# Graph layer on one core: every product of the last stage in plain fp32, from thirteen buffers

## The reference

```python
def _lap_mul(A, x):
    d = 1.0 / jnp.sqrt(jnp.sum(A, axis=-1))
    return d[:, None] * (A @ (d[:, None] * x))

z = leaky_relu(_lap_mul(A, x) @ W1 + b1, 0.1)
d2 = maximum(sq[:, None] + sq[None, :] - 2.0 * (z @ z.T), 0)     # sq = sum(z*z)
S = exp(-sqrt(d2 + 1e-10) / 2)
S = where(rank of S in its row < 4, S, 0)
x = _layernorm(x + _lap_mul(S + A, x) @ W2 + b2)
```

## Time and profile before

| | |
|---|---|
| median without a profile | 2692.08 us (3 runs) |
| span of the profiled execution | 2759.5 us |
| TensorE busy in it | 2482.6 us (90%) |
| VectorE busy | 2319.8 us (84%) |
| ScalarE busy | 1606.7 us (58%) |
| GpSimd busy | 1195.4 us (43%) |
| moved by DMA | 718.58 MB, 260 GB/s in the mean |

### The profile page before, as it was taken

One profiled execution on the slowest core, in us unless ns is written; L12 is line 12 of the kernel. 1 busy time (PEld: TensorE's weight loads), 2 busy tenths in 40 slices (PEclk: granted clock), 3 DMA queues, 4 the chain that ended last, 5 costly groups with the idle time before them and its releaser, 6 DMA issues.

```text
span 2759.5 us, 29107 instructions
## 1 busy us (share of the span) xinstructions
PE 2482.6 (90%) x9356; PEld 1722.4 (62%) x9356; DVE 2319.8 (84%) x1411; ACT 1606.7 (58%) x1905; POOL 1195.4 (43%) x987
## 2 busy tenths in 40 slices
PE   1367999999999998899999999999999987888978
PEld 0133444444677776578787877778787764666655
DVE  7998899977788888999999999999999773666766
ACT  0000000000477767999989899899988763555655
POOL 0000000000000000377778878788878956666760
PEclk9688999999999999999999999999999988999989
DMA  9999999995899960146555655555655688988975
GB/s 385 421 402 408 398 421 421 421 421 215 320 349 342 338 226 7 35 141 183 151 163 138 179 142 175 140 170 149 174 143 167 182 309 343 347 324 320 345 295 208
DMA packets 147949, 718.58 MB, mean 260 GB/s; under 512 B 19025, under 2 KB 26961, under 8 KB 86609
## 3 DMA queue, kind: packets, MB, share of 16 engines
q1 hardware_dynamic: 124384, 670.49, 65.6%
q0 software_dynamic: 18800, 37.77, 5.7%
q10 hardware_dynamic: 4608, 8.39, 0.8%
HBM read 680.40 MB, written 36.18 MB: 260 GB/s over the span
## 4 chain that ended last, share of the span: by engine, by line
PE 56%; issue 10%; ACT 10%; DVE 9%; DMA 7%; POOL 3%; another core or an unknown queue 3%; SPq 0%; ACTq 0%; POOLq 0%; DVEq 0%
PE PS L767 17%; PE PS L866 5%; PE PS L868 5%; PE PS L867 5%; DMA ring<-at 4%; ACT R L1141 3%; PE PS L834 3%; PE PS L910 3%; PE PS L921 3%; PE PS L911 3%; PE PS L830 2%; PE PS L831 2%; ACT ah_t L1191 2%; DVE R L1621 2%
## 5 line engine op out<-in xcount | busy, mean ns | idle before, releaser
L1299 POOL TENSOR_TENSOR al<-ring,ah 128x1024 fp32r<-128x1024 f32 x264 | 644.0, 2441 | 180.5 <-ACT ah L1112 168.7
L1621 DVE MAX8 R<-R 128x8 f32<-128x8192 f32 x64 | 555.9, 8685 | 68.1 <-ACT R L1141 67.9
L1141 ACT ACTIVATE R<-PS 128x1024 f32<-128x1024 f32 x512 | 518.1, 1018 | 114.1 <-PE PS L874 83.1
L1624 DVE FIND_INDEX8 R<-R,R 128x8 uint32<-128x8192 f32 x64 | 555.9, 8685 | 0.3 <-issue 0.3
L1272 POOL CAST zst<-zh 128x128 fp32r<-128x128 f32 (+1 forms) x64 | 26.2, 410 | 1113.2 <-DVE zl L1556 811.5
L866 PE MATMUL PS<-zh,zst 128*128 128x512 f32 x1024 | 407.3, 398 | 28.6 <-ACT PS L1127 12.7
L868 PE MATMUL PS<-zh,zst 128*128 128x512 f32 x1024 | 400.4, 391 | 0.0
L867 PE MATMUL PS<-zl,zst 128*128 128x512 f32 x1024 | 400.1, 391 | 0.0
L1456 POOL DMA_INDIRECT R<-xs_dram,R x256 | 279.7, 1093 | 145.2 <-issue 75.5
L1127 ACT ACTIVATE PS<-R 128x1024 f32<-128x1024 f32 x310 | 318.0, 1026 | 6.6
L1046 ACT ACTIVATE tiny<-rowsum 128x4 f32<-128x4 f32 x16 | 3.3, 205 | 481.2 <-DVE rowsum L1491 481.2
(11 more groups left out here) (177 smaller groups left out, 4469.9 us busy)
## 6 DMA issues: line engine op xcount, KB each, us to landing
R<-at SPq DMA_DIRECT2D x152, 1024.0 KB, 13.3
ring<-at SPq DMA_DIRECT2D x148, 1024.0 KB, 9.5
ring<-at SPq DMA_DIRECT2D x264, 512.0 KB, 3.9
cache<-at SPq DMA_DIRECT2D x117, 1024.0 KB, 20.2
raw_sq<-at SPq DMA_DIRECT2D x21, 1024.0 KB
raw_z<-at SPq DMA_DIRECT2D x20, 1024.0 KB
raw_ring<-at SPq DMA_DIRECT2D x20, 1024.0 KB
acc_dram<-R POOLq DMA_DIRECT2D x78, 256.0 KB, 5.7
```

Of the source, the lines that this page charges most:

```text
L1141: act.activation(score[j % 2][:, c * EC:(c + 1) * EC].rearrange("p (b c) -> p b c", b=2), pair(first, j, c), ACT.Copy).then_inc(copied, 1)
L1299: pool.tensor_tensor(al[:, k % SPLIT], raw[k % RAW], ah[:, k % SPLIT].bitcast(F32), ALU.subtract)\
L1621: v.max(top[:, j], score[j % 2]).then_inc(dve3, 1)
L1624: v.max_index(place[:, j], top[:, j], score[j % 2]).then_inc(placed, 1)
```

## The change

All 124 quads of the last stage are multiplied as the plain ones were.
- `round_t`, `rest_t`, the two subtractions on GpSimd, `ah_t`, `al_t` and their semaphores are gone. A quad's product waits for its load and for x.
- For h < 14 x comes from `xs_t`, 32 KB per partition in the place of `zh`. It is filled from `xp_dram`, which holds the scaled x of a group in one piece. In the loop one store of it takes the place of the stores of the two halves, and SP waits for both stores before it loads the next rows of x into `xg`. GpSimd's wait for the stores of the halves is gone; the halves are still made, for the pieces.
- `RAW_T` is 13: four buffers in `R1`, four in the place of `zl`, one over `sqn`, four in the ring. The load of quad u waits for the product of quad u - 13. The opening sequence of SP's loads is written out anew, by which part of `z` and of the ring is free. `ACC_AT` moves from (9, 20, 40) to (16, 27, 47).
- The last chain of small steps starts where it did, with no subtraction between its steps.

The diff, without the lines that only remove semaphores and names:

```diff
-RAW_T = 6
-BY_POOL = 2
-RESTS = 2
+RAW_T = 13
+CHAIN_AT = 2
...
-OPEN_T, SUM_AFTER, ACC_AT = 6, 4, (9, 20, 40)
+OPEN_T, SUM_AFTER, ACC_AT = 6, 4, (16, 27, 47)
...
-        ah_t = [sb(f"ah_t{k}", [P, TB, BC], F32R, at=top_of["ring"] + k * SLOT * 4) for k in range(2)]
-        al_t = [sb("al_t0", [P, TB, BC], F32R, at=top_of["ring"] + 2 * SLOT * 4),
-                sb("al_t1", [P, TB, BC], F32R, at=top_of["R1"] + 3 * SLOT * 4)]
+        xs_t = sb("xs_t", [P, T, D], at=top_of["zh"])
+        raw_t = [R1[:, k * SLOT:(k + 1) * SLOT].rearrange("p (k c) -> p k c", c=BC) for k in range(4)]
+        raw_t += [sb(f"raw_z{k}", [P, TB, BC], at=top_of["zl"] + k * SLOT * 4)[:, :, :] for k in range(4)]
+        raw_t.append(sb("raw_sq", [P, TB, BC], at=top_of["sqn"])[:, :, :])
+        raw_t += [sb(f"raw_ring{k}", [P, TB, BC], at=top_of["ring"] + k * SLOT * 4)[:, :, :] for k in range(4)]
...
-                        dst = xh_dram[bass.ds(g, 1)].rearrange("o p t d -> p (o t) d")
-                        sp.dma_start(dst, xgh_g[:, :, :].bitcast(F32)).then_inc(s_split, 16)
-                        dst = xl_dram[bass.ds(g, 1)].rearrange("o p t d -> p (o t) d")
-                        sp.dma_start(dst, xgl_g[:, :, :].bitcast(F32)).then_inc(s_split, 16)
+                        dst = xp_dram[bass.ds(g, 1)].rearrange("o p t d -> p (o t) d")
+                        sp.dma_start(dst, xg).then_inc(s_xp, 16)
                     if k == RAW + (NP0 // 2 if first else 0):
                         sp.wait_ge(s_xg, 16 * (g + 1))
+                        sp.wait_ge(s_xp, 16 * (g + 1))
                         sp.dma_start(xg, x[:, bass.ds((g + 1) * GT, GT)]).then_inc(s_xn, 16)
...
             def load_t(u):
                 b, h = tail[u]
-                if u >= RAW_T and plain[u - RAW_T]:
+                if u >= RAW_T:
                     sp.wait_ge(prod_t, u - RAW_T + 1)
-                elif u >= RAW_T:
-                    wait_rest(sp, u - RAW_T)
                 sp.dma_start(raw_t[u % RAW_T], at[b, h]).then_inc(ld_t[u % RAW_T], 16)
...
+                sp.dma_start(xs_t[:, g * GT:(g + 1) * GT], xp_dram[g]).then_inc(s_xs[g], 16)
+
+            def wait_z_free(chunks):
+
+                sp.wait_ge(gram, NE * (T - 1) + chunks)
+
+            sp.wait_ge(s_xp, 16 * (G - 1))
             sp.wait_ge(placed, T - 1)
...
+            load_t(0)
+            wait_z_free(1)
+            load_xs(0)
+            load_t(1)
             load_t(2)
-            sp.wait_ge(gram, NE * T)
+            wait_z_free(2)
+            load_xs(1)
             load_t(3)
+            load_t(4)
+            wait_z_free(4)
             load_xs(2)
-            load_t(4)
+            load_t(5)
+            load_xs(3)
+            wait_z_free(6)
+            load_t(6)
+            wait_z_free(8)
+            load_t(7)
+            load_t(8)
+            load_xs(4)
             sp.wait_ge(prodb, pieces_before(G - 1))
-            load_t(5)
+            for u in range(9, RAW_T):
+                load_t(u)
+            load_xs(5)
+            load_xs(6)
...
-                if plain[u]:
+                pe.wait_ge(ld_t[u % RAW_T], 16 * (u // RAW_T + 1))
+                if h >= LAST:
                     pe.wait_ge(xg_ok, chain_of(G - 1, False))
...
+                else:
+                    pe.wait_ge(s_xs[h * TB // GT], 16)
                 for k in range(TB):
...
+                    of_x = xg[:, (h * TB + k) % GT] if h >= LAST else xs_t[:, h * TB + k]
+                    i = pe.matmul(bank, of_x, raw_t[u % RAW_T][:, k], start=from_zero and k == 0,
+                                  stop=last and k == TB - 1, skip_group_check=True)
                 i.then_inc(prod_t, 1)
...
             for u in range(len(tail)):
-                if not plain[u]:
-                    round_t(u)
...
-            for u in range(BY_POOL):
-                pool.wait_ge(rnd_t, u + 1)
-                pool.tensor_tensor(al_t[u % 2][:, :, :], raw_t[u % RAW_T], ah_t[u % 2][:, :, :].bitcast(F32),
-                                   ALU.subtract).then_inc(al_pool, 1)
...
-                if not plain[u]:
-                    rest_t(u)
```

More of the change, by code:

```diff
@@ L126, in plan_tail, with build @@
     return quads
-def build(nc, x, at, W1, b1, W2, b2, consts, out, xs_dram, xh_dram, xl_dram, acc_dram):
+def build(nc, x, at, W1, b1, W2, b2, consts, out, xs_dram, xp_dram, acc_dram):
     loads, products, two = plan_ab()
@@ L284, in build @@
         spare = R2[:, (B - 1) * BC:B * BC]
[L285 to L292, removed]
-        ah_t = [sb(f"ah_t{k}", [P, TB, BC], F32R, at=top_of["ring"] + k * SLOT * 4) for k in range(2)]
-        al_t = [sb("al_t0", [P, TB, BC], F32R, at=top_of["ring"] + 2 * SLOT * 4),
-                sb("al_t1", [P, TB, BC], F32R, at=top_of["R1"] + 3 * SLOT * 4)]
+        xs_t = sb("xs_t", [P, T, D], at=top_of["zh"])
[3 more added lines that the diff above has]
+        raw_t += [sb(f"raw_ring{k}", [P, TB, BC], at=top_of["ring"] + k * SLOT * 4)[:, :, :] for k in range(4)]
+        assert len(raw_t) == RAW_T
         bt = [N]
@@ L376, in build @@
         flushed = sem("flushed")
-        s_split = sem("s_split")
+        s_xp = sem("s_xp")
         s_xs = [sem(f"s_xs{k}") for k in range(G - 1)]
@@ L521, in build @@
         n_heavy = [f + 1 - n_light[f] for f in range(B)]
[L523 to L537, removed]
         def wait_yf(eng, f):
@@ L966, in quad @@
                     pe.wait_ge(yf_heavy, b - HB - 1)
-                if plain[u]:
+                pe.wait_ge(ld_t[u % RAW_T], 16 * (u // RAW_T + 1))
+                if h >= LAST:
                     pe.wait_ge(xg_ok, chain_of(G - 1, False))
[L969 to L978, removed]
-                for k in range(TB):
[L980 to L988, removed]
+                else:
+                    pe.wait_ge(s_xs[h * TB // GT], 16)
+                for k in range(TB):
+                    of_x = xg[:, (h * TB + k) % GT] if h >= LAST else xs_t[:, h * TB + k]
+                    i = pe.matmul(bank, of_x, raw_t[u % RAW_T][:, k], start=from_zero and k == 0,
+                                  stop=last and k == TB - 1, skip_group_check=True)
                 i.then_inc(prod_t, 1)
@@ L1239, in _ @@
                         seed_heavy(i)
-                if u == BY_POOL:
+                if u == CHAIN_AT:
                     s_of_distances(G - 1)
-                if u == BY_POOL + 1:
+                if u == CHAIN_AT + 1:
                     root_of_sums(G - 1)
@@ L1660, in _ @@
             lt = Link(v, dve4, 0)
-            def rest_t(u):
-                n = place_of[u]
-                v.wait_ge(rnd_t, n + 1)
-                wait_halves_free(v, u)
-                for part_ in range(RESTS):
-                    ks = slice(part_ * TB // RESTS, (part_ + 1) * TB // RESTS)
-                    v.tensor_tensor(al_t[n % 2][:, ks], raw_t[u % RAW_T][:, ks], ah_t[n % 2][:, ks].bitcast(F32),
-                                    ALU.subtract).then_inc(al_dve, 1)
             def light_sum(b):
@@ L1720, in _ @@
             last_chain_a(lk)
-            for u in range(BY_POOL, len(tail)):
-                if u == BY_POOL + 1:
+            for u in range(CHAIN_AT, len(tail)):
+                if u == CHAIN_AT + 1:
                     last_near_sums(lk)
-                if u == BY_POOL + 2:
+                if u == CHAIN_AT + 2:
                     last_scale_of_rows(lk)
                     scale_last_xg(G - 1)
-                if not plain[u]:
-                    rest_t(u)
                 for b in LIGHTS:
@@ L1767 @@
     xs_dram = nc.dram_tensor("xs_dram", (N, D), F32, kind="Internal").ap()
-    xh_dram, xl_dram = (nc.dram_tensor(n, (G, P, GT, D), F32, kind="Internal").ap() for n in ("xh_dram", "xl_dram"))
+    xp_dram = nc.dram_tensor("xp_dram", (G, P, GT, D), F32, kind="Internal").ap()
     acc_dram = nc.dram_tensor("acc_dram", (len(ROWS_0), P, BC), F32, kind="Internal").ap()
-    build(nc, **ins, out=out, xs_dram=xs_dram, xh_dram=xh_dram, xl_dram=xl_dram, acc_dram=acc_dram)
+    build(nc, **ins, out=out, xs_dram=xs_dram, xp_dram=xp_dram, acc_dram=acc_dram)
     r = run_bass_kernel_spmd(nc, [arrays], core_ids=[0])
```

22 lines of the change are left out of this document (removed).

## The result

The changed kernel takes 2716.99 us (median of 4 runs, 2713.03 to 2720.10) against 2693.72 us for the kernel before on the same chip (4 runs, 2691.94 to 2695.66). The ratio is 1.0087, 95% interval 1.0075 to 1.0099: 23 us slower. 2712 us were forecast, in a range from 2688 to 2726 us.

The account below looks back on a forecast made before the run. TensorE was taken to pace the changed last stage: 453.8 us of work plus 3 and 1.5 us, less a 0.9 us earlier start, against 437.8 us before, +19.6 us. Rounded up, 2692.1 + 20 = 2712 us, range 2688 to 2726 us.

Parts of the forecast that it names:

- Two times of one stage: Last stage before: 67.4 us exist only under the profiler, so its true length is 437.8 us, not 505.2.
- Part 1: TensorE's products, last stage: a plain quad costs 0.67 us more than a halved one, +61.6 us; 453.8 us in all.
- Part 2: Rounding and subtraction, last stage: removing them can win only TensorE's 45.6 us of waits for halves.
- Part 3: Opening of the last stage: start 0.9 us earlier, 3 us wait for `xg`, 1.5 us lower clock; stage 458.3 us.
- Part 4: Last-stage transfers: busy share falls to 0.88, thirteen buffers cover 45 us; no charge, bounds 0 and 8 us.
- Part 5: GpSimd's gathers, last stage: 355 us for 256 gathers against 458 us of path; no charge.
- Part 6: Loop before the last stage: one store replaces two, TensorE stays 98% busy; 0 us, bounds -3 and +3.
- Real stalls: Rival: ScalarE's 77.6 us of last-stage waits are the kernel's own, giving 2644 us; 0.15 together with a partial case.
- it comes out even: Rival: a third of the 67.4 us outside the last stage, or a loop gain; within 5 us of before; 0.09.
- Transfers as the bound: Rival: last-stage gathers and loads leave TensorE short, up to 8 us more, 2727 us with the second length; 0.12.
- The clock: Rival: the clock falls under plain fp32, so every quad costs up to twice as much; 0.01.
- The sum: Whole kernel: 458.3 - 0.9 - 437.8 = +19.6 us, or +26.5 us with the second length of the stage before.

Follow-up runs that it names:

- half loads: Kernel before, but from the seventh quad on each halved quad loads only two of its four tiles, all waits and products kept; 2684.00 us in one run.
- run of half the products: Changed kernel, but each quad with h < 14 is multiplied with only two of its four tiles; 2662.13 us, ratio 0.9888.
- after_again: Changed kernel with no edit, measured and profiled a second time; 2718.14 us, ratio 1.0100 against the kernel before.
- seven buffers: Changed kernel with `RAW_T` = 7 instead of 13, stored sums loaded at the same quads; 2712.56 us, ratio 1.0073.
- two mixtures: Kernel before with the quads of the first three or four groups of x plain, seven or eight raw buffers; 2705.49 and 2708.26 us.

## Why the prediction was right

- *Two times of one stage.* Right, and shown: the second profiled execution has no such waits, and a stage of 436.6 us where 437.8 was worked out. What held the engines in the first, the profiler or something else, is not shown; no run counts it.
- *Part 1.* Right. Quads follow each other every 3.43 us and `gathered` takes 0.89 us; 453.8 us of TensorE's own work, by the prediction's count. One slip is in that count: the stage ends with the last quad, and two of the 32 calls come behind it (`gathered` at 2704.27 us and a `times_w2` at 2705.85), so inside it are 30, 26.7 us. Both sums have 1.8 us too many, which cancels in the difference: 452.0 us after, 390.4 before. The rule of the Trainium skill, page "FP8 and Floating Point Precision", section "TensorE Precision Notes", four passes for true fp32 against three fp32r products here, leads the right way; as an estimate from it 4/3 of 2.76 us would make 3.68 us, and the measurement, 3.43 us, decides. A quarter of one plain product is 3.43 / 16 = 0.214 us here, less than the 0.23 us of an fp32r product.
- *Part 2.* Right in its size: 44.4 us above TensorE's own work in the stage before, 45.6 forecast (46.2 and 47.4 by the count of 30 calls). Its cause was too narrow. It called them "TensorE's waits for halves". Of the 46.2 us, 13.7 lie in the first six quads, 9.9 in quads 6 to 23 and 22.5 behind. The middle ones are transfers that come late, as the half loads show. Of the last, 7.9 go by changing ScalarE's order alone, and 14.6 stay unexplained. The 13.7 us are not taken apart either; a part is not waiting at all, since the granted clock in these six quads was 0.83 (2244.90 to 2275.20 us, TensorE busy 22.03 of 30.30). That did not touch the sum, because the change takes away ScalarE's and VectorE's part in the stage as a whole: TensorE's stage after is only 459.4 - 452.0 = 7.4 us over its own work, all causes together.
- *Part 3.* The stage was put at 458.3 us and measured 459.4. The wait for `xg` is 3.3 us (3 forecast), with both of its ends some 2 us later than put: TensorE was there at 2265.74 us instead of 2263.6, and the scaling over at 2268.88 instead of 2266.6. The clock was priced too low for this execution: quad 6 takes 6.31 us instead of 3.43, 2.9 us more where 1.5 stood (bounds 0 and 3.4). It is no fixed price: the same quad took 5.20 us in `after_again` and 3.51 us with seven buffers. It is the stretch behind the wait, at a granted clock of 0.83:

```profile
2269.02 6.47 PE L955 MATMUL PS<-raw_z,R 128*128 128x512 f32 x8 [3.28 <-DVE R L1604]
...
2260.00:2280.00 20.00, 16.72 (x33) 7.10 (x32) 5.51 (x15) 3.23 (x5) 2.02 (x2) 0.83 1.02 421
```
  The first quad starts at 2244.90 us, not 0.9 earlier than before. That hides a term that was put too low, not too high. Counted from the start of the last record of distances, the first quad comes 3.88 us later in all seven executions that round it first (2244.94 - 2241.07 in the second profile of the kernel before), and 2.04 us later in this one (2244.90 - 2242.87), 2.0 to 2.6 us in all four executions of the changed kernel and its variants: 1.3 to 1.8 us earlier. But the loop ends at another time in each execution, so that the first quad starts between 2241.9 and 2248.9 us in the twelve of the experiments, and one profile can't show the term in the total.
- *Part 4.* No charge was right; its reason was off. The share was put at 0.88, below 0.9; it is 0.92, and 1.00 from 2300 to 2650 us. With thirteen buffers the loads run ahead, and the share falls only at the end of the stage. Its own sign of being wrong, "TensorE's idle time ends on a load", is absent in this execution and there in `after_again`, with 0.5 us inside the stage for rows of x and 1.9 us, handed on through VectorE, for stored sums: within the bounds of 0 to 8 us, and without effect on the length of the stage. What decides is 406 us of transfers against 459 us of path.
- *Part 5.* Right: no `gathered` call waits, and each takes its 0.89 us.
- *Part 6.* Right: 1016.94 against 1017.62 us in the same 1040.
- *The rivals.* Real stalls (2644 us), and with them "it comes out even", fell with the second profile of before. Transfers as the bound (2727 us) fell with the run of half the products. The clock is 1.00 from 2300 us on.
- *The sum.* +20 us forecast, +23.3 measured. The stages differ by 459.4 - 436.6 = 22.8 us where 20.5 were put: the one before is 1.2 us shorter, the one after 1.1 us longer (the clock 1.4 and the wait 0.3 more, the two calls behind the end 1.8 less, and 1.2 more spread over the rest). The forecast took the first of its two lengths of the stage before, 437.8 us; the second, 430.9, would have given +26.5, and the measured 436.6 lies nearer the first. The 0.9 us of an earlier start did not show in the total, for the reason above.

## What to carry to other kernels

Before you take work off ScalarE and VectorE by giving TensorE more of it, add up TensorE's own time in that stage before and after: the stalls there are all that can be won, here some 45 us for 62 us. If the stalls are the aim, look first in the timeline at what the waiting engine's producer does ahead of its product: one rounding moved ahead of the closing work gave 7 us; three pairs of buffers, which left only four raw ones, and two mixtures made the kernel slower. And where span and unprofiled time of a kernel differ by 2%, take a second profile before any wait is priced.

## What was not expected of the hardware

- A profiled execution can be 67 us longer than the kernel (2759.5 us of span against 2692.08), all of it in the last stage, with waits called "remote" and without landing times of the loads. Each of the thirteen other profiled executions of this study, in part of the same kernel, lay within 7 us of the median of its own kernel, so the first was the exception.
- A busy share of 1.01 did not mean that the queues set the pace. With 86 loads halved, at a share of 0.83, the last 99 distances of the stage were the same within 0.1 us, and with another order on ScalarE they shrank by 7.9 us in all with every load in place.
- Plain fp32 has a small price: a quad of four products of 128 x 512 takes 3.43 us plain and 2.76 us as twelve fp32r products, a ratio of 1.24.
